# An audio tower on one NeuronCore: overflow groups of 64 tokens instead of 32, each residual just ahead of its scatter, and constant matmuls after the attention

## What is computed

```python
h = _L0_tok_ref(x, ...)                       # x is (4, 750, 128); sign convolution, h is (4, 748, 64)
h = h + _L0_attn_ref(_layernorm(h), ...)      # 8 heads; scores (748 x 748), softmax over the first token axis,
...                                           #   only the diagonal of attn weighs v; then W0
h = h + _L0_ffn_ref(_layernorm(h), ...)       # a tree of depth 7: 255 nodes with weights of their own

for _ in range(DEPTH + 1):                    # the tree, for each token t
    score = jnp.einsum('td,td->t', flat_x, w1s[current]) + b1s[current]
    choice = ((jnp.sign(score) + 1.0) / 2.0).astype(jnp.int32)
    current = current * 2 + choice + 1
path_weights = jax.nn.gelu(jnp.abs(logits), approximate=False)
for i in range(DEPTH + 1):
    t_i = jnp.einsum('td,tdo->to', flat_x, w2s[nodes_i]) + b2s[nodes_i]
    out = out + t_i * path_weights[:, i][:, None]
```

## Time and profile before

| | |
|---|---|
| median of 3 runs | 483.22 us (482.93 to 486.01) |
| the profiled execution | 478.25 us |
| its span, first to last instruction | 476.4 us |
| mean granted clock of PE | 0.908 |
| busy: PE, DVE, ACT, POOL | 75%, 72%, 68%, 58% |
| attention and sorting | 0 to 361 us |
| fixed tiles | 365 to 420 us |
| overflow tiles | 420 to 470 us |

### The profile page before, as it was taken

One profiled execution on the slowest core, in us unless ns is written; L12 is line 12 of the kernel. 1 busy time (PEld: TensorE's weight loads), 2 busy tenths in 40 slices (PEclk: granted clock), 3 DMA queues, 4 the chain that ended last, 5 costly groups with the idle time before them and its releaser, 6 DMA issues. The chain is left out here.

```text
span 476.4 us, 8299 instructions
## 1 busy us (share of the span) xinstructions
PE 357.5 (75%) x2588; PEld 251.8 (53%) x2588; DVE 344.1 (72%) x588; ACT 325.3 (68%) x832; POOL 276.7 (58%) x389
## 2 busy tenths in 40 slices
PE   1167898867898898778898668993313998989990
PEld 1144666645555564546664446662212776768880
DVE  0466869898888888997888997788720887864552
ACT  1455988788798898659797667678000887778771
POOL 4325762785868777676589661661462577863221
PEclk9997989999999999887999998795555999999997
DMA  4434342519969943031254120017915022200000
GB/s 94 128 79 118 97 100 56 122 35 197 217 144 180 158 98 97 17 81 34 65 117 113 26 73 1 1 42 113 119 36 150 12 56 58 51 12 11 7 8 8
DMA packets 58954, 37.28 MB, mean 78 GB/s; under 512 B 31661, under 2 KB 57607, under 8 KB 58906
## 3 DMA queue, kind: packets, MB, share of 16 engines
q1 hardware_dynamic: 54778, 33.81, 34.8%
q0 software_dynamic: 3328, 2.36, 2.0%
q10 hardware_dynamic: 800, 0.49, 0.5%
HBM read 11.42 MB, written 7.50 MB: 40 GB/s over the span
## 5 line engine op out<-in xcount | busy, mean ns | idle before, releaser
L1238 ACT ACTIVATE Z<-Z,nm 125x748 f32<-125x748 f32 x192 | 166.1, 870 | 64.4 <-DVE nm L1438 63.1
L1438 DVE TENSOR_REDUCE nm<-Z 125x1 f32<-125x748 f32 x192 | 175.7, 933 | 40.4 <-PE Z L964 34.3
L964 PE MATMUL Z<-pool_a 128*125 128x512 f16 (+1 forms) x768 | 168.2, 349 | 25.7 <-ACT Z L1238 22.0
L964 PEld LDWEIGHTS Z<-pool_a 128*125 128x125 f16 x768 | 92.2, 145 | 70.4 <-ACT Z L1238 43.1
L750 POOL DMA_INDIRECT out<-pre,va x44 | 43.4, 987 | 39.8 <-DVE pre L1744 31.7
L1738 DVE TENSOR_REDUCE pre<-va 128x64 f32<-128x512 f32 x44 | 45.5, 1035 | 9.1 <-ACT va L1321 4.7
L817 PE MATMUL Z<-xhT,wq 128*128 128x249 f16 (+1 forms) x192 | 33.1, 293 | 11.3 <-DVEq L1449 9.9
L1238 ACT ACTIVATION_READ_ACCUMULATOR Z<-Z,nm 125x1 f32 x192 | 40.9, 213 | 0.0
L668 POOL DMA_INDIRECT sorted_rows<-xrow,slot x24 | 29.4, 1223 | 18.7 <-DVE slot L1611 12.1
L628 POOL TENSOR_TENSOR va<-va 125x256 f32<-125x256 f32 (+2 forms) x54 | 29.6, 548 | 8.9 <-DVE va L1468 5.8
L1342 ACT COPY va<-Z 32x455 f32<-32x455 f32 x48 | 25.3, 526 | 8.6 <-PE Z L1102 5.6
(11 more groups left out here) (252 smaller groups left out, 642.4 us busy)
## 6 DMA issues: line engine op xcount, KB each, us to landing
pool_a<-pool_a SPq DMA_DIRECT2D x64, 187.0 KB, 3.3
pool_a<-pool_a SPq DMA_DIRECT2D x64, 93.5 KB, 2.2
sorted_rows<-zrow SPq DMA_DIRECT2D x1, 3640.0 KB, 21.3
va<-sorted_rows SPq DMA_DIRECT2D x12, 260.0 KB, 3.9
w<-in_L_ffn_w2s SPq DMA_DIRECT2D x1, 2048.0 KB
pre<-in_x SPq DMA_DIRECT2D x4, 375.0 KB
pool_a<-in_L_ffn_w2s SPq DMA_DIRECT2D x1, 1024.0 KB
out<-pre,va POOLq DMA_INDIRECT x44
```

What stands on the lines that cost most here:

```text
L964: last = mm(z[0:XP, c0:c1], kst[:, u % 3, a, hd, KST[t]:KST[t] + XP], qst[:, u % 3, hd, c0:c1], start=(a == 0), stop=(a == 1))
L1238: sc_.activation(z, z, ACT.Exp, bias=nm[0:XP, u % 4, i:i + 1], accum_out=sm[0:XP, u % 4, i:i + 1]).then_inc(s_exp, 1)
L1438: v.tensor_reduce(nm[0:XP, u % 4, i:i + 1], Z[n % 3][0:XP, 0:N], X, ALU.max, negate=True).then_inc(s_max, 1)
```

## The change

Three things change.

1. Overflow groups have G2 = 64 slots; a tile has two. OVG stays 96, so there is room for 48 overflow tiles instead of 24, 80 tiles in all, and the transfer that empties `sorted_rows` grows with them. PE and ACT work on two groups for each tile. `leaf_counts`, `old_terms` and `group_slots` count in units of 64. A word of `lam4` now serves two tiles, and 8 words are loaded ahead instead of 12. The sections are nested: each is inside the `If` of the one before.
2. POOL adds the residual of tile k directly before the scatter of tile k, where it did that of tile k + 1 first.
3. `keep_awake(n)` issues n matmuls of 128 x 512 bf16 on constants (`tri`, `pathb`) into bank Z1, which nobody reads before it is written anew. They stand at five steps of the last four rounds, between the loads of the leaves, and before and after a new wait for the landed scatters (`s_segs`).

```diff
+G2 = 64
...
-SLOTS = STAT + OVG * G
-ST_TILES, OV_TILES = STAT // P, OVG * G // P
+SLOTS = STAT + OVG * G2
+ST_TILES, OV_TILES = STAT // P, OVG * G2 // P
...
+        def sections(engine, groups, work, m=ST_TILES // 4, end=F_TILES // 4):
+
+            if m < end:
+                with engine.If(groups > 2 * (4 * m - ST_TILES)):
+                    work(m)
+                    sections(engine, groups, work, m + 1, end)
...
-            residual(0)
             for k in range(ST_TILES):
-                if k + 1 < ST_TILES:
-                    residual(k + 1)
+                residual(k)
                 rows_out(k)
...
+            def keep_awake(n):
+
+                for _ in range(n):
+                    mm(Z[1][:, 0:4 * P].rearrange("p (r c) -> p r c", r=4), tri[:],
+                       pathb[:].unsqueeze(1).to_broadcast([P, 4, P]), start=True, stop=True)
+
+            AWAKE = {(0, 2): 18, (0, 8): 3, (1, 6): 14, (2, 0): 9, (2, 2): 9}
...
                     for f in fills(u, i):
                         fill(f)
+                    if (u - NU, i) in AWAKE:
+                        pe.wait_ge(s_exp, 2 * NT * NU)
+                        keep_awake(AWAKE[u - NU, i])
...
                 n = k - ST_TILES
-                for g in range(4):
-                    if n:
-                        pe.wait_ge(s_yv, 4 * (n - 1) + g + 1)
-                    elif g % 2 == 0:
-                        bank_ready(ST_TILES + g // 2)
-                    y = OWN[g][0:G]
-                    xg = xk[:, G * g:G * (g + 1)]
-                    own = leaves >> 7 * g if g else leaves
-                    leaf = nc.tensor.snap(own & LEAVES - 1 if g < 3 else own)
+                for h in range(2):
+                    g = 2 * n + h
+                    if g >= 4:
+                        pe.wait_ge(s_yv, g - 3)
+                    elif h == 0:
+                        bank_ready(ST_TILES + n)
+                    y = OWN[g % 4][0:G2]
+                    xg = xk[:, G2 * h:G2 * (h + 1)]
+                    own = leaves >> 7 * (g % 4) if g % 4 else leaves
+                    leaf = nc.tensor.snap(own & LEAVES - 1 if g % 4 < 3 else own)
...
+            keep_awake(5)
             pe.wait_ge(s_goff, 1)
-            early = [load_leaves(k) for k in range(ST_TILES, ST_TILES + EARLY)]
+            early = []
+            for j in range(EARLY):
+                early.append(load_leaves(j))
+                keep_awake(3)
+            keep_awake(14)
+            pe.wait_ge(s_segs, 16 * TT)
+            keep_awake(11)
             pe.wait_ge(s_tab, 16 * 2)
...
+            def section_gates(m):
+                for k in range(4 * m, 4 * m + 4):
+                    n = k - ST_TILES
+                    if n >= 2:
+                        act.wait_ge(s_wy, k - 1)
+                    for h in range(2):
+                        act.wait_ge(s_y, banks(k) + h + 1)
+                        yw = yv[h * G2:(h + 1) * G2, k % 2].rearrange("p h l o -> p (h l o)")
+                        sc_.copy(yw[:, E1:DEPTH * E1], OWN[(2 * n + h) % 4][0:G2, 0:7 * E1]).then_inc(s_yv, 1)
+                    act.wait_ge(s_y, banks(k) + 3)
+                    sc_.copy(yv[:, k % 2, 0, 0, :], ROOT[k % 2][:, 0:E1]).then_inc(s_y0, 1)
...
-                link(v.tensor_scalar(ogi[:, 0:1], col[:, c_new0], -1.0, float(G - 1), ALU.add, ALU.max))
-                link(v.tensor_scalar(ogi[:, 1:2], ogi[:, 0:1], 5, None, ALU.arith_shift_right))
+                link(v.tensor_scalar(ogi[:, 0:1], col[:, c_new0], float(G2 - G - 1), float(G2 - 1), ALU.add, ALU.max))
+                link(v.tensor_scalar(ogi[:, 1:2], ogi[:, 0:1], 6, None, ALU.arith_shift_right))
```

More of the change, by code:

```diff
@@ L751, in rows_out, with section_out @@
                                       bounds_check=T - 1, oob_is_err=False).then_inc(s_outr[k % NO], 16)
-            residual(0)
             for k in range(ST_TILES):
-                if k + 1 < ST_TILES:
-                    residual(k + 1)
+                residual(k)
                 rows_out(k)
-            for m in range(ST_TILES // 4, F_TILES // 4):
-                with pool.If(groups > 4 * (4 * m - ST_TILES)):
-                    for k in range(4 * m, 4 * m + 4):
-                        rows_out(k)
+            def section_out(m):
+                for k in range(4 * m, 4 * m + 4):
+                    rows_out(k)
+            sections(pool, groups, section_out)
         @block.tensor
@@ L1121, in _, with section_products @@
             groups = pe.value_load(nact[0:1, 0:1], min_val=0, max_val=OVG)
-            for m in range(ST_TILES // 4, F_TILES // 4):
-                with pe.If(groups > 4 * (4 * m - ST_TILES)):
-                    for k in range(4 * m, 4 * m + 4):
-                        n = k - ST_TILES
-                        overflow_products(k, early[n] if n < EARLY else load_leaves(k))
-                        if k % 4 == 1 and k + 4 < F_TILES:
-                            xs_T(m + 1)
+            def section_products(m):
+                for k in range(4 * m, 4 * m + 4):
+                    j = (k - ST_TILES) // 2
+                    if k % 2 == 0:
+                        leaves = early[j] if j < EARLY else load_leaves(j)
+                    overflow_products(k, leaves)
+                    if k % 4 == 1 and k + 4 < F_TILES:
+                        xs_T(m + 1)
+            sections(pe, groups, section_products)
         @block.scalar
@@ L1581, in group_slots @@
                 z = zone(("pf", b))
[L1582 removed]
+                link(v.tensor_scalar(col[:, c_new], z[:, 0:1], float(G2), float(STAT + 1), ALU.mult, ALU.add))
                 link(v.tensor_copy(col[:, c_end], z[:, 1:2]))
@@ L1750, in _, with section_sums @@
             groups = dve.value_load(nact[0:1, 0:1], min_val=0, max_val=OVG)
-            for m in range(ST_TILES // 4, F_TILES // 4):
-                with dve.If(groups > 4 * (4 * m - ST_TILES)):
-                    for k in range(4 * m, 4 * m + 4):
-                        weigh(k)
-                        sum_levels(k)
-                        add_residual(k)
+            def section_sums(m):
+                for k in range(4 * m, 4 * m + 4):
+                    weigh(k)
+                    sum_levels(k)
+                    add_residual(k)
+            sections(dve, groups, section_sums)
 _INS = ["x", "L0_tok_kernel", "L0_tok_bias", "L0_tok_beta", "L0_tok_moving_mean", "L0_tok_moving_var",
```

46 lines of the change are left out of this document (16 added, 30 removed).

## The result

The changed kernel takes 481.2 us, the median of 12 runs (478.0 to 484.4); the kernel before, on the same chip, 478.5 us (473.9 to 486.0), the median of 12 runs, among them the three of the table ahead of the prediction. The ratio is 1.0075, 95% interval 1.0048 to 1.0102: no change by the bound of the prediction, a little slower, where 471.8 us (a ratio of 0.976) was forecast. Every ratio in this document leaves out runs over 1.5% above the fastest of the same kernel, here three of the kernel before, so it is not the quotient of the medians.

The account below looks back on a forecast made before the run. The prediction saw three stretches: overflow tiles paced by PE, a serial chain before the fixed tiles at half clock, and the attention's emptying transfer. From 483.22 us, -8.1 and -3.3 gave 471.8; own range 468 to 478, whole range 465.5 to 479.

Parts of the forecast that it names:

- The emptying transfer: SP's queue in the attention: emptying 80 tiles instead of 56 delays nothing, 0; ends 0 and 9.1 us.
- Rival 4: Attention: the longer emptying transfer holds up unit 6 by its full 9.1 us, giving 480.9 us; 4%.
- Residual before scatter: POOL's fixed tiles: waiting for the add just made costs below 0.3 us a tile, 0 on the path.
- The main term: Overflow tiles at the kernel's end: groups of 64 instead of 32 save 8.1 us.
- Overflow tiles: Kernel's end: a group of 64 costs what one of 32 does; 15 steps of 2.2 us, -8.1 us.
- Matmuls on constants: PE from the last rounds to the fixed tiles: constant matmuls keep its clock full, -3.3 us.
- Full clock from 327 us to the end: Sign expected in the new profile: PE's granted clock full from about 327 us to the end.
- the first eighteen: Constant matmuls before "pf", where PE idled 6.41 us: they take 5.9 us and are just hidden.
- rival 2: PE's clock never rises there, so constant matmuls delay its work: +5.6 us, giving 480.7 us; 6%.
- Transposes and the clock: PE between constant matmuls: transposes may not count as clock activity, so they help nothing and rival 1 (20%) gains chance.

Follow-up runs that it names:

- s3_old_pool: Changed kernel with POOL's old order of residuals and scatters, 80 tiles still emptied; ratio 0.9793 to the kernel before.
- e4: Kernel before with only POOL's new order of residual and scatter; ratio 1.0018 to the kernel before.
- t1_split: Changed kernel with POOL's old order, 56 tiles emptied in unit 5, the other 24 behind unit 10's stacks; 465.3 us, ratio 0.9697.
- t2_split_ten: t1_split with ten constant matmuls instead of fourteen ahead of the last "pf"; ratio 0.9697 to the kernel before.
- v1_fill56: Changed kernel emptying only 56 tiles, POOL's new order kept, on a chip of kind B; ratio 0.9781 to the kernel before.
- s1_after: Changed kernel unchanged, run again on a chip of kind A; ratio 0.9903 to the kernel before.
- e7: Changed kernel emptying 56 tiles, with POOL's old order and no constant matmuls; 459.2 us, ratio 0.9770 to the kernel before.
- e6: Changed kernel emptying 56 tiles and with POOL's old order, constant matmuls kept; 456.1 us, ratio 0.9687 to the kernel before.
- e8: Kernel before, unchanged, profiled again on a chip of kind A; 470.3 us.
- e5: Changed kernel unchanged, profiled a second time, on e8's chip; ratio 0.9889 to the kernel before.
- s4_both: Changed kernel emptying 56 tiles and with POOL's old order, constant matmuls kept, on another chip of kind A; ratio 0.9676 to the kernel before.
- t3_after: Changed kernel unchanged, on another chip of kind B; 480.8 us, ratio 1.0052 to the kernel before.

## Why the prediction was wrong

On the first chip the forecast of the last scatter was 11.5 us sooner, and it came 4.9 later. By the table the 16 us between them are 9.3 in the attention, 13.7 in the overflow tiles (7.2 more instead of 6.5 less) and 0.4 at the two short steps, less 7.1 in the fixed tiles. Two steps of the prediction failed, both terms that it put at 0.

**The emptying transfer, taken at 0: the step that failed first.** The low end of its range was taken for the reason that the transfer "was through some 10 us ahead" of unit 6. What was read was the landing of the transfer; what counts is when the stacks behind it land. The issue at 118.6 us already took 8.3 us in the kernel before, where the same four copies for the unit before took 2.5 us, and the stacks have to travel after it:

```profile
102.32 2.54 SPq L389 DMA_DIRECT2D pool_a<-pool_a  x4
...
118.59 8.27 SPq L389 DMA_DIRECT2D pool_a<-pool_a  x4
```

Measured: 9.3 us late at the last score product on the first chip, 5.1 us in the mean of all profiles (4.1 without s3_old_pool's), 5.5 +- 2.4 and 1.0 +- 2.8 us in the timed pairs, the second of which does not tell it from nothing. Rival 4 (480.9 us, 4%) named the mechanism and its price; its time is within 0.3 us of the result by luck: it has the gain of 8.1 in the overflow tiles, which on this chip was a loss of 7.2, and not the 7 us of stalls that went.

**Residual before scatter, 0 on the path: the step that failed second,** in its size and its cover. The wait for an add just made is 0.79 us where it was 0.17, so 0.62 more and not under 0.3, and the fixed tile on POOL went from 1.5 us to 2.15. The step said that POOL has 12 buffers "to run behind" and that the last scatter is "an overflow one, untouched". A queue in order touches it all the same: 32 x 0.65 = 21 us of backlog go into the overflow tiles, and what they can take back is 16 x (2.2 - 1.28) = 15. By this estimate 6 us remain; measured on kind A it is about 7 (7.4 to 9.2 us from DVE's last add to the last scatter, against 0.8); with the old overflow tiles it would have been 12 x (3.67 - 1.28) = 29, which is why e4 lost nothing. The main term itself had taken the cover away, and I asked only what is late next of PE, DVE and ACT.

**A cost not in the list.** On kind B PE's 14 us of single products cover POOL's backlog, so it is not added to it: there the last scatter again comes 0.8 us after DVE's last add. No rival had it. That it comes from POOL's row of scatters is argued from where it stands and from t1_split and t2_split_ten, which have neither (nor the long transfer, but v1_fill56 has the stretch without that); why it happens is open.

**Overflow tiles, -8.1: right on kind A.** A step is 33.2 / 15 = 2.21 us on four chips of kind A, for 2.2 predicted; a group of 64 is 0.83 us on PE (425.65 to 426.48 in s1_after) and 530 ns on ACT, near the 0.81 and 0.53 that were taken. Alone, the groups gave a ratio of 0.977 (e7), 10.8 us +- 2.1, a little more than the term. On kind B this holds with the old order only (32.2 and 33.4 us for the 15 steps in the two split kernels).

**Matmuls on constants, -3.3: right in size, by another way.** Measured 3.1 to 3.9 us (e7 against e6: medians, and ratios). Full clock from 327 us to the end was wrong, and the first eighteen took 6.6 us for 5.9. The term's own sum is off as well: 3.1 + 0.75 with one "sl" (0.85) still slow is 3.0, not 3.3, and the range's upper end, from -3.1 and -0.5, is 479.6 and not 478; neither decides the outcome. In the changed kernel's profile the clock is full for the first node products, 1.59 us instead of 2.84, and for "sl" (342.99 to 344.27), and falls again behind it:

```profile
345.34 0.50 PE L939 MATMUL Z<-pre,pathb 128*128 128x375 bf16 x1 [0.73 <-DVE slf L1642]
345.63 5.75 PE L1035 MATMUL Z<-pathb,tri 128*128 128x512 bf16 x14
351.21 0.17 PE L945 MATMUL Z<-db,tri 128*128 128x1 bf16 x1
```

The fourteen ran mostly at half clock and held "pf" up by 1.5 us, which is rival 2's cost at one of its places. From the last score product to SP's load 2.3 us were gained, and on kind A 2.0 us more in the fixed tiles, which start at full clock (53.4 us in e7, 51.4 in e6).

**Transposes and the clock.** The prediction had cited the Trainium skill ("TensorE: Matmul & The Clock Gate", "Part 4: PE-mode transpose") for transposes not counting as activity of PE the way matmuls do. The clock fell at the end of a stretch that held transposes and products (340.13 to 344.1); no run here had the transposes alone changed, so it stays undecided.

**The fixed tiles.** Of the 9.5 us gained there on the first chip, about 3 are the clock and the sooner first overflow tile, as on kind A (54.4 us in e8, 51.5 in e5) and near the 2.4 predicted. The other 7 are the stalls, which on kind B stand in all three profiles with POOL's old order and in none of the three with the new one, and which no step of mine had; a gain by luck that the stretch on PE gave back twice over.

Together, on kind A (e5 and e8, the same chip): attention +0.9, to the load -2.3, fixed tiles -2.9, overflow tiles -7.7, behind them +8.4, in sum -3.6 us. With both edits taken back, or the transfer split, the forecast's 0.976 is reached and passed: 0.968 (0.965 to 0.970) in s4_both, 0.970 in t1_split on kind B.

## What to carry to other kernels

Shortening a stage takes away the time in which another engine's queue catches up: before costing an edit at 0 because an engine may run behind, add up its whole queue to the last instruction, with the new pace of the others. A large transfer put ahead of small ones in one queue delays them, so read when the small ones behind it are issued and land, not when it lands; put later (t1_split), the extra part delayed nothing that the profile shows. And a result on one chip can hide or invent a per cent: so a comparison of one per cent wants more than one chip.

## What was not expected of the hardware

- A scatter that waits for the add just made by the same engine waits 0.79 us; where the add just made is the next tile's it waits 0.17, and a scatter behind a scatter 0.30.
- Two kinds of chips: the kernel before takes 470 to 472 us on four and 478 to 481 on three. On the second kind PE runs single products about a microsecond apart, for 14 us, while POOL issues result scatters back to back (three profiles of three with that pattern, none of eight such profiles on the first kind). Why is open. The Trainium skill, "Runtime: NRT & Kernel Launch", section "Instruction fetch mechanics", says that an engine fetches its instructions in blocks through a DMA queue of its own, and that a taken branch can force a fetch. The stretch does begin at a branch, the last section's; but in t3_after the trace has no packet of the two instruction queues between 450.5 and 464 us, and no run changed the branches, so this is neither shown nor excluded. Nor was the nesting of the sections, which all kernels with groups of 64 have, ever taken back alone.
- SP is held up in the issue of small copies behind a large one: four copies of 93.5 KB took 2.5 us to issue with nothing large ahead, 8 to 11 behind 3640 KB, 18 to 21 behind 5200 KB.
- After idle times of the same length at unit 6 (2.23 and 2.26 us) the granted clock of PE fell in one kernel (0.83 over 140 to 160 us) and stayed at 1.00 in the other.
